# Each engine's order as a written list of steps and items, ring tiles by item, no identity products

## The reference

```python
h = x + attention(rms(x), rms(x), sa_w*)          # 16 heads of 16, 256 keys
h = h + attention(rms(h), context, ca_w*)         # 16 heads of 16, 77 keys
h = h + (silu(rms(h) @ w_gate) * (rms(h) @ w_up)) @ w_down   # inner size 1024
F = layernorm(h); X = layernorm(context)
a = softmax(F @ X.T / 16) @ X
c = gelu(a @ fc1.T + b1) @ fc2.T + b2
n = layernorm(c)
out = F + gamma2 * (c + gamma1 * (softmax(n @ n.T / 16) @ n))
```

## Time and profile before

| | |
|---|---|
| runs | 936.92, 936.81, 940.48 us; median 936.92 |
| profiled execution | span 938.1 us from first to last instruction; the profile gives no other time of it |
| PE busy | 869.7 us (93%), 8114 products |
| PEld busy | 738.1 us (79%) |
| DVE, ACT, POOL busy | 666.7, 546.2, 252.9 us |
| chain that ended last | PE 74%, DVE 12%, ACT 6%, issue 3%, DMA 2% |
| DMA | 71.73 MB, mean 76 GB/s |

### The profile page before, as it was taken

One profiled execution on the slowest core, in us unless ns is written; L12 is line 12 of the kernel. 1 busy time (PEld: TensorE's weight loads), 2 busy tenths in 40 slices (PEclk: granted clock), 3 DMA queues, 4 the chain that ended last, 5 costly groups with the idle time before them and its releaser, 6 DMA issues.

```text
span 938.1 us, 21220 instructions
## 1 busy us (share of the span) xinstructions
PE 869.7 (93%) x8114; PEld 738.1 (79%) x8114; DVE 666.7 (71%) x1445; ACT 546.2 (58%) x1098; POOL 252.9 (27%) x511
## 2 busy tenths in 40 slices
...
PEclk9899999999999999999999999999999999997999
...
GB/s 207 191 148 128 134 76 81 61 105 26 57 101 43 94 64 80 79 81 56 102 38 55 104 44 95 63 81 77 80 55 92 50 43 105 43 33 35 17 12 23
DMA packets 74660, 71.73 MB, mean 76 GB/s; under 512 B 17633, under 2 KB 67409, under 8 KB 74561
## 3 DMA queue, kind: packets, MB, share of 16 engines
...
...
## 4 chain that ended last, share of the span: by engine, by line
PE 74%; DVE 12%; ACT 6%; issue 3%; DMA 2%; SPq 1%; POOL 1%; ACTq 0%; DVEq 0%
PE mring L1527 21%; PE ring L1527 12%; PE down_ps L1667 9%; PE od L1634 9%; PE ring L1620 7%; PE ring L1600 6%; DVE mx_sa L1296 4%; PE ring L1535 2%; PE mring L1696 1%; PE mring L1769 1%; DVE late_a L1343 1%; ACT probs L1094 1%; PE ring L1607 1%; PE mring L1677 1%; DMA pk_sa<-qkT 1%
## 5 line engine op out<-in xcount | busy, mean ns | idle before, releaser
L1094 ACT ACTIVATE probs<-ring 128x1024 f32<-128x1024 f32 (+1 forms) x192 | 190.9, 1022 | 45.3 <-PE ring L1620 41.5
L849 POOL TENSOR_TENSOR hidT_lo<-late_a,hidT_hi 128x256 fp32r<-128x256 f32 x128 | 95.8, 750 | 316.9 <-ACT hidT_hi L1121 315.7
L1296 DVE TENSOR_REDUCE mx_sa<-ring 128x4 f32<-128x1024 f32 x128 | 153.4, 1215 | 11.4 <-PE ring L1600 11.3
L1301 DVE TENSOR_REDUCE mx_ca<-ring 128x4 f32<-128x308 f32 x128 | 55.1, 474 | 59.8 <-PE ring L1600 59.7
L1349 DVE SCALAR_TENSOR_TENSOR late_a<-late_a,mring 128x256 f32<-128x256 f32 x128 | 52.9, 413 | 49.1 <-ACT late_a L1111 48.7
L1667 PE MATMUL down_ps<-down_hi,hidT_hi 128*128 128x256 f32 x256 | 79.0, 309 | 0.0
L1111 ACT ACTIVATE late_a<-mring 128x256 f32<-128x256 f32 x128 | 48.4, 378 | 51.2 <-PE mring L1527 48.9
L1600 PE MATMUL ring<-pk_sa 63*128 63x256 f32 x512 | 62.8, 329 | 14.9 <-DVE mx_sa L1296 6.4
L1667 PE MATMUL down_ps<-down_lo,hidT_hi 128*128 128x256 f32 x256 | 71.3, 279 | 0.0
L1667 PE MATMUL down_ps<-down_hi,hidT_lo 128*128 128x256 f32 x256 | 71.3, 279 | 0.0
L1121 ACT ACTIVATE hidT_hi<-late_a 128x256 fp32r<-128x256 f32 x128 | 52.6, 413 | 27.0 <-DVE late_a L1351 19.9
...
## 6 DMA issues: line engine op xcount, KB each, us to landing
pk_sa<-qkT SPq DMA_DIRECT2D x96, 256.0 KB, 2.8
qpk_ca<-qkT SPq DMA_DIRECT2D x48, 256.0 KB, 2.6
x_sb<-x SPq DMA_DIRECT2D x16, 256.0 KB, 2.8
x_res<-x SPq DMA_DIRECT2D x16, 256.0 KB, 3.0
out<-o_sb SPq DMA_DIRECT2D x16, 256.0 KB, 2.2
...
```

What stands on the lines that cost most here:

```text
L849: nc.gpsimd.tensor_tensor(hidT[1][:, m % HID, :], hid[:, m % 2, :], hidT[0][:, m % HID, :].bitcast(F32), ALU.subtract).then_inc(S["hidlo"] ...
L1094: nc.scalar.activation(granule(g, tag)[0:rows_, i0:i0 + 2, :, :].rearrange("p i h t -> p h i t"), ring_tile(("E", tag, k))[0:rows_].rearra ...
L1296: nc.vector.tensor_reduce(mx[tag][:, :, :, k].rearrange("p q h -> p h q"), ps[:].rearrange("p h (q t) -> p h q t", t=T), AX_X, ALU.max).th ...
L1301: nc.vector.tensor_reduce(mx[tag][:, :, half, 2 * C * (k % 2) + k // 2:2 * C * (k % 2) + k // 2 + C + 1:C].rearrange("p q i -> p i q"), v, ...
```

## The change

`ORDER` is now a full list for every engine: `gu.6@9` means step gu.6 of item 9, and `sequence` only reads the words. `MOVED` is gone. `NAMES` lists the steps of an engine in the old order, from which the rings' users and their usual tiles come. `IDLE` is empty, so no identity product is issued. `MOVED_TILES` names steps and items that use the other tile of `ring` or `mring` (30 pairs of step and item of `ring`, 62 of `mring`); all functions that name a tile now pass the item too. The list of steps is the same, in number and kind, as are the operations and their shapes.

```diff
 ORDER = {
     "sp": """
-        mr.sa@0 wl.2@11 sk.0@1 sv.0@2 sk.4@-2 vl.ca@-1 ls@8 cl.4@-1 pq.ca@-1 mr.ca@-1 wl.10@-1 sv.4@-3 ldx@2 sk.1@0 cl.1@3 pqk.sa.0@1 wl.4@26 cl.3@0 sv.1@1
+        wl.0@0 wl.1@0 wl.4@0 wl.2@0 wl.6@0 wl.8@0 wl.3@0 wl.7@0 wl.5@0 cl.0@0 wl.9@0 ldx@0 ls@0 ldx@1 lb@0 cl.1@0 pqk.sa.0@0 sv.0@0 cl.2@0 pqk.sa.1@0
...
-    size = len(STEPS[engine])
-    places = []
-    for k, (step, ahead) in enumerate(STEPS[engine]):
-        shifts = MOVED.get((engine, ".".join(map(str, step))), {})
-        for n in range(1 if step[0] in ONCE else B):
-            places.append((n - ahead + (k + 0.5) / size + shifts.get(n, 0), k, step, n))
-    return [(step, n) for _, _, step, n in sorted(places)]
+    words = (word.rsplit("@", 1) for word in ORDER[engine].split())
+    return [(step_of(name), int(n)) for name, n in words]
+
+STEPS = {e: [step_of(name) for name in NAMES[e].split()] for e in NAMES}
...
-IDLE = {
-    ("gk.0", 0): 18, ("S.sa.7", 0): 4, ("maxT.sa", 0): 3, ("E.sa.0", 0): 11, ("S.sa.0", 1): 7, ("S.sa.7", 1): 5, ("E.sa.0", 1): 4,
-    ("E.sa.2", 1): 1, ("E.sa.7", 1): 2, ("e2", 13): 5, ("gu.0", 15): 5, ("nFT", 15): 7, ("fT", 14): 3, ("f2", 14): 12, ("s2", 15): 4,
-    ("mT2", 15): 3, ("e2", 15): 2,
-}
+IDLE = {}
...
+MOVED_TILES = {
+    "ring": """
+        T.sa@0 qk.sa@0,1,11 S.sa.2@0 S.sa.3@0,1,4 S.sa.4@0 maxT.sa@0 v.sa@0 E.sa.7@0,15 wo.ca@2,14 S.ca.2@3,4,13 S.ca.3@3,4,13,14 S.ca.1@7 E.sa.5@8
...
+def tile_at(ring, step, n):
+
+    tiles, _, used = RINGS[ring]
+    return TILES.get((ring, step, n), used.index(step) % tiles)
...
-            tile = used.index(step) % tiles
+            tile = tile_at(ring, step, n)
```

435 lines of the change are left out of this document (264 added, 171 removed), and 70 rows, old and new, of the table MOVED.

## The result

The changed kernel took 951.75 us (median of four runs, 949.26 to 955.84), the kernel before 938.7 beside it: ratio 1.0144, 95% interval 1.0105 to 1.0183. It is slower by 1.4%; forecast were 921 us and a range of 906 to 935.

A forecast was written before the change was run, and what follows sets the result against it. PE was taken to bound the middle, chains through engines and DMAs the start and end. 938.1 - 7.8 - 3.8 - 5 - 2.5 + 2.5 = 921.5, less 1.2 from profile to median, said as 921 us; range 906 to 935.

The forecast's parts named there:

- the start: Up to item 0's E: x first, q and k and S earlier, lead carried along; 7.8 us gained, bounds 0 and 12.
- the middle: The twelve items that PE bounds: row switches 3.8 us and the stretch of the maxima 5 us gained.
- the end: After gu.7@15: dnp.3@15 to dnp.7@15 come ahead of the wait for item 14's sides; 2.5 us gained, bounds 0 and 4.
- The identity products: Leaving them out lowers the clock a little: 1.5 us lost at the start, 1 us at the end.
- the 24 us below: Upper bound on the loss from missing identity products, pointing to the slower-clock rival's price.
- Slower: the clock: Rival, chance 0.08: without identity products the clock stays low in the first 100 and last 90 us; 943 us.
- the maxima's stretch: DVE's gapless stretch in each item begins earlier with dnp.3 moved into it: 0.4 us an item, 5 us, bounds 0 and 10.
- The other moves: Other small reorderings of steps, priced at nothing because PE has other steps around them.
- Row switches: On PE, nearly all in the middle: 349 switches in place of 391, 0.09 us each, 3.8 us gained, bounds 0 and 3.8.
- The marks: Signs in the profile after that would show the forecast right: item period, v's wait, dnp.7@15's distance to gu.7@15, early clock.

The follow-up runs named there:

- e1: The kernel before with its 96 identity products left out, order and tiles unchanged: 950.4 us, ratio 1.0114.
- e10: The changed kernel with 122 identity products at pauses of its own order near the start and end: 937.3 us, ratio 0.9988 to the kernel before.
- e6: The kernel before, identity products kept, with only PE's dnp.3 moved behind pv.ca.0 in twelve items: 940.4 us, ratio 1.0014.
- e13: e10 with T.mlp ahead of xn.ca on DVE (eight items) and vl.ca ahead of the packing DMAs on SP (two items): 930.2 us.
- e7: The kernel before, identity products kept, with only PE's dnp.4 moved behind wo.sa in ten items: 942.2 us, ratio 1.0030.
- e9: The changed kernel with POOL's first memsets waiting until DVE has written item 0's normed rows: 954.0 us, ratio 1.0165 to the kernel before.
- e15: The kernel before with new start and last 30 PE steps, identity products at their pauses, POOL's first memsets behind item 0's normed rows: 932.9 us.

## Why the prediction was wrong

Set part by part against the sum: the start was to give 6.3 us (7.8 less 1.5 for the clock) and gave 3.9; the middle was to give 8.8 and took 10.9; the end was to give 1.5 (2.5 less 1) and took 6.6. So of some 30 us between forecast and result 19.7 lie in the middle and 10.5 at the two ends. Two steps failed: the price of the identity products, and in the middle the two gains together with all other moves, which the forecast had put at nothing.

**The identity products** are the first step that failed. The forecast put "1.5 us at the start" and "1 us at the end"; they are worth some 12 us in the order of before (e1) and 14.4 in the new one, at its own pauses (e10). The reason it gave for so little, "Where PE did little the clock fell all the same", misread: in these two stretches PE was busy for 6.04 and 7.00 of 7 us. And it read them the wrong way round: the 33 us at the lower level were what was left with the products in place, not what would be there without. The windows of before could not show the other side, and I took a price where I had no row for it. The bound was there ("the 24 us below"), but with 0.08 for it. The rival "Slower: the clock" named the mechanism and the places, and with 943 was 9 short: it kept the 8.8 us of gain in the middle, where the changed kernel lost 10.9, 7.3 of it in pauses and 3.4 at the lower clock.

**The middle** is the second, and the larger. First the maxima's stretch (5 us). PE's wait ahead of v did fall (6.5 to 1.7), but not by moving dnp.3 (e6: 6.5). "With that DVE's stretch can begin up to 0.67 earlier" holds for its first step only: the second needs S.sa.0, which dnp.3 delays by as much as it had delayed pv.ca.0. I had followed the wait that was to go and not asked what the next step of the same engine would wait for. Against 4.8 us less there and 2.8 less ahead of S stand new waits of 4.9, 3.8, 3.5 and 3.2 us: the sum of the pauses went from 12.8 to 20.1. The other moves, which "I price at nothing", were moves in PE's list alone; two of these waits came from DVE's list (xn.ca ahead of T.mlp) and SP's (vl.ca between packing DMAs), of which the forecast says nothing. Mending these two takes the middle from 584.5 to 574.1 us and the time from 937.3 to 930.2 (e13).

**Row switches** (3.8 us): the 0.09 compares a step of S with a step of E. Like with like, in the middle of before, from a step's start to the next one's (pauses taken off), E.sa takes 0.35 us ahead of another S or E and 0.39 ahead of 128 rows, S.sa 0.43 and 0.44. The rest of the middle is 555.8 against 555.6 with 32 switches fewer in it, so nothing of the 3.8 is seen. In e7, with 16 fewer, the rest fell by 0.3, and PE then met a result that wasn't there yet.

**The start** (7.8 us): q and k were forecast "near 14.3" and came at 16.89, S.sa.0@0 "near 25.5" and came at 27.8, E.sa.0@0 "near 41" and came at 44.5. The context's DMA landed at 14.7 (e9), nearly as forecast (13.5 to 14); what I had not seen is that POOL's memsets had moved beside DVE's first multiplications (7.10 us). The 24 products of q and k took 4.8 us (forecast 5.3, before 3.2). The lead was there, 9.7 at E.sa.7@0, and 10.9 at item 3 in e10; without identity products the clock took all but 3.7.

**The end** (2.5 us) has the right size, 2.4 in the table above, but mostly not from the place that the forecast named, and that is luck: of the "at least 2 us" between gu.7@15 and dnp.7@15 1.0 came, and none in e15; 2.1 came ahead of gu.7@15, where nothing was forecast. In the changed kernel the clock turned it into a loss of 6.6. Timeline of PE after, answering to the earlier trace rows: the last product of dnp.7@15 and xT@14.

```profile
922.40 0.28 PE L1694 MATMUL down_ps<-down_hi,hidT_lo 128*128 128x256 f32 x1
...
923.10 0.65 PE L1767 MATMUL ring<-ident,sides 128*65 128x128 f32 x4 [0.29 <-DVE sides L1491]
```

xT@14 stands behind dnp.7@15 and waits 0.29 instead of 1.74, as forecast. But dnp.3@15 (0.7 us) now stands behind gu.7@15 too, and dnp.6@15 waits 0.63 for the low part of its input.

**The marks** that I had set: period near 51.0 (52.7), v's wait under 0.3 (up to 0.54), dnp.7@15 at least 2 us closer to gu.7@15 (1.0), granted clock of 0.9 in the first 100 us (0.82 in the mean, 0.93 before, and 0.5 from 78.6 to 95.7). The last is what the forecast itself had called proof against it.

**Slips of the working**, none of which decides: twice the 2.86 us of twelve products is 5.7, not 5.3; 921.5 less 1.2 is 920.3; dnp.3 is six products, some 0.8 us in all, not two of 0.39.
